# Cross attention: weights loaded a stage earlier, biases as one-row products, values placed by ScalarE

## The chip, the cores and the metric

The kernel runs on one core of a Trainium2 chip, in one launch. The metric is the device time of one execution in microseconds (us), lower is better. TensorE (PE) multiplies, VectorE (DVE), ScalarE (ACT) and GpSimd (POOL) work on vectors, SyncE (SP) issues most of the transfers. Each engine runs its own instruction list in order, and semaphores order the engines among each other.

## The reference, cut to what matters

Four gated layers run one after the other on x of 4x256x256, each one an attention-like part and a feed-forward part. The third attention-like part is the cross attention that the change touches; ahead of it stands a mixture of 16 experts with top-2 routing.

```python
x = x + jnp.tanh(g_ffn[1]) * _L1_ffn_ref(_layernorm(x, axis=-1), ...)            # 16 experts: stage 3
x = x + jnp.tanh(g_xattn[2]) * _L2_xattn_ref(_layernorm(x, axis=-1), ctx_1024, ...)  # stage 4
...
y_dca = y[:, -DCA:, :]                       # the last 16 of 256 context rows
y_main = y[:, :-DCA, :]
kv_dca = (y_dca @ Wkv_dca + bkv_dca).reshape(b, DCA, 2, H, HD)
k_dca = _ln(kv_dca[:, :, 0], kn_dca_w, kn_dca_b)
v_dca = kv_dca[:, :, 1]
q = _ln((x @ Wq + bq).reshape(b, s1, H, HD), qn_w, qn_b)
kv = jnp.concatenate([y_main @ Wk + bk, y_main @ Wv + bv], axis=-1)
kv = kv.reshape(b, s2, H, 2 * HD)
k = _ln(kv[..., :HD], kn_w, kn_b)
v = kv[..., HD:]
ctx = _attn(qT, k..., v...)                  # softmax over the 240 main rows
ctx_dca = _attn(qT, k_dca..., v_dca...)      # softmax over the 16 others
return (ctx + DCA_WEIGHT * ctx_dca) @ Wo + bo
```

There are 16 heads of 16 columns; `_ln` normalises each head's 16 numbers. All of it is float32.

## The kernel before, in words

The program is a chain of stages, each a block in which every engine has its own list, with all engines meeting between the blocks. Stage 3 is the mixture of 16 experts (`sparse_moe`), stage 4 the cross attention (`stage4`). The 1024 tokens are 8 tiles of 128 rows; a tile is called t, a batch of 256 rows b is two tiles. SBUF is split into large regions (regA, regC, regD), from which an `Arena` hands out pieces in order.

Stage 3 begins with a layer norm, the routing, a store of the normalised rows to DRAM (`h_rows`, issued by SP) and their gather by expert (POOL, L1373). It ends with the gathers of the results (L1379), the last additions to x on DVE (L1638, L1640) and ScalarE's two copies of weights for stage 5 (L1064, L1066). SP's list at its start is two weight loads for stage 5 (`load_w5`, L1032 and L1033) and then the two `h_rows` stores (L1354).

Stage 4 starts with a preparation and goes over into a loop over 64 heads. The preparation is what the change touches:

- SP issues fifteen loads, the weights wkv, wdca, wq and wo and the biases and norm weights spread over 128 partitions (L1710 to L1724).
- POOL copies the context's odd tiles into `ctxm` (main rows, zeros elsewhere) and `ctxd` (the 16 other rows, zeros elsewhere; L1738 to L1741), clears the padding of `qpad` and `kpad` (L1743), and sets the columns of ones (L1749, L1755).
- DVE and ScalarE do the layer norm of x (`norm_on_vector`, L145 to L158), PE turns it (`turn_on_tensor`, L175) and ScalarE copies it to `hT` (L1817).
- PE projects keys and values for two tiles per batch (`project_kv`: one 128x512 product for an even tile, L1888; two for an odd one, L1890 and L1891) and queries (`project_q`: four 128x256 products per batch, L1898). ScalarE copies each result from PSUM (`keep_kv` L1797, `keep_q` L1801). PE's order is kv(0), kv(1), the transposes of h, q(0), then kv, kv, q of batches 1, 2 and 3.
- POOL adds the biases in SBUF (`add_biases`, L1760 and L1762) and places the values with their row mask into `vaug` (`place_values`, L1772), the right-hand factor of the last product of the attention, together with the columns of ones.
- DVE normalises the heads: `center_heads` (L2030 to L2034), then ScalarE's squares (L1806), `variances` (L2038, L2042), ScalarE's root (L1811), `scale_heads` (L2048, L2050), `affine_heads` (L2058, L2060) and `pads` (L2071, L2073), which write `kpad` and `qpad` as float32r parts. ScalarE's list has the squares of batch 0 behind `keep_q(1)`.
- Once all four batches are projected and kept (`s_kve` 8, `s_qe` 4), PE turns the keys of batch 0 (`turn_heads`, L1919), ScalarE copies them (L1834) and then does the squares of batch 1; DVE normalises batch 1 and takes the maxima of the scores of batch 0 (L2082). From there on the order is a slot list written out by hand, 16 slots per batch.

Inside the head loop 13 scan steps of another layer ("late" steps) are woven in; their buffers lie over pieces that only the preparation uses (`early`), so SP, POOL and ScalarE wait for the preparation before the first of them.

## Time and profile before

| | us |
|---|---|
| median of 3 runs | 985.37 |
| lowest and highest of them | 981.57, 985.49 |
| the profiled execution | 986.16 |
| its span | 984.4 |
| mean granted TensorE clock | 0.821 |
| busy: PE, DVE, ACT, POOL | 679.4, 724.4, 333.7, 194.9 |

Times in the profile count from the span's start. Stage 3 lies at about 351 to 481, stage 4 begins at 483.0, its head loop at about 566. A line of a timeline is: start, duration, engine, line of the kernel, operation, out<-in, number of instructions, and in brackets how long the engine had been idle before and what released it. In the profile an engine is busy while it executes; waits are inferred from semaphores. A matmul's recorded duration overlaps the next one's, so its price in a sequence is the distance between starts.

### The profile page before, as it was taken

How to read it: one execution, taken by the hardware profiler on the slowest of the kernel's cores; microseconds unless marked ns; L12 is line 12 of the kernel's file. 1: busy time of each engine (PE TensorE's matmuls, PEld its weight loads, DVE VectorE, ACT ScalarE, POOL GpSimd, SP SyncE). 2: the span in 40 equal slices, each digit the busy share in tenths (PEclk: the TensorE clock that was granted, in tenths of full speed). 3: DMA queues.
4: the chain of work that ended last, by engine and by line, in shares of the span. 5: the costliest groups of instructions: out<-in, count | busy, mean ns of one | idle time of the engine just before them, and what ended most of it. 6: DMA issues, size and time to landing. Idle time of an engine off the chain costs nothing. (4 is left out here: it accounts for less than half of the span.)

```text
span 984.4 us, 9448 instructions
## 1 busy us (share of the span) xinstructions
PE 679.4 (69%) x3040; PEld 447.3 (45%) x3043; DVE 724.4 (74%) x1379; ACT 333.7 (34%) x534; POOL 194.9 (20%) x168
## 2 busy tenths in 40 slices
PE   4419989999945434898273388988861443489997
PEld 2304545555534333566142255555440222477775
DVE  5997798979866765966438769788849886945554
ACT  4004517455213311231232265555620322423221
POOL 0000001112200003343478000000104121204441
PEclk9758999999977665999586589789885675579999
DMA  9300003434574031453400033423625000000000
GB/s 238 90 12 0 6 0 65 85 65 85 88 198 138 0 129 43 112 126 93 108 16 0 0 86 78 91 58 75 139 45 202 0 1 0 10 0 1 22 1 22
DMA packets 39538, 62.22 MB, mean 63 GB/s; under 512 B 5010, under 2 KB 24090, under 8 KB 38210
## 3 DMA queue, kind: packets, MB, share of 16 engines
q1 hardware_dynamic: 28530, 38.68, 13.6%
q0 software_dynamic: 10960, 22.94, 12.7%
q8 instruction: 25, 0.41, 0.2%
q14 instruction: 23, 0.19, 0.1%
HBM read 38.54 MB, written 6.29 MB: 46 GB/s over the span
## 5 line engine op out<-in xcount | busy, mean ns | idle before, releaser
L519 PE MATMUL ps<-hT,regA 128*128 128x512 f32 x256 | 115.3, 593 | 1.0 <-ACT hT L435 1.0
L1975 PE MATMUL ps<-regD,regC 128*34 128x256 f32 x256 | 74.1, 416 | 23.2 <-ACT regD L1840 11.8
L519 PEld LDWEIGHTS ps<-hT,regA 128*128 128x128 f32 x256 | 48.4, 190 | 51.9 <-issue 46.8
L690 POOL DMA_DIRECT2D yssm<-regB x19 | 22.9, 1208 | 246.5 <-DVE regB L642 236.0
L530 PE MATMUL ps<-regA,regC 128*128 128x256 f32 x256 | 64.3, 396 | 6.9 <-DVE regC L649 5.4
L1149 POOL TENSOR_TENSOR w_lo<-regA,w_hi 128x768 fp32r<-128x768 f32 x22 | 42.6, 1940 | 100.1 <-ACT w_hi L1111 100.1
L530 PEld LDWEIGHTS ps<-regA,regC 128*128 128x128 f32 x256 | 47.9, 194 | 31.9 <-DVE regC L649 20.7
L1373 POOL DMA_INDIRECT regA<-h_rows,regA x31 | 30.1, 970 | 141.2 <-DVE regA L1593 110.9
L445 ACT ACTIVATE regC<-ps 128x512 f32<-128x512 f32 x32 | 19.1, 597 | 92.8 <-PE ps L519 88.1
L1840 ACT ACTIVATE regD<-ps 128x512 f32<-128x512 f32 x64 | 38.1, 596 | 32.9 <-PE ps L1961 32.1
L1287 DVE TENSOR_TENSOR regB<-regB,ps 128x512 f32<-128x512 f32 x22 | 15.1, 688 | 45.8 <-ACT regB L1129 45.8
L1975 PEld LDWEIGHTS ps<-regD,regC 128*34 128x34 f32 x256 | 24.8, 117 | 48.2 <-issue 18.9
L634 DVE TENSOR_TENSOR_SCAN regB<-regB 128x512 f32<-128x512 f32 x38 | 44.5, 1213 | 2.8
L1788 POOL DMA_DIRECT2D yssm<-regC x13 | 15.7, 1211 | 136.1 <-DVE regC L2123 114.4
L2082 DVE TENSOR_REDUCE regC<-ps 128x4 f32<-128x960 f32 x64 | 39.8, 685 | 3.9 <-PE ps L1930 3.9
L1919 PE MATMUL ps<-ident,regA 128*128 128x128 f32 x192 | 32.3, 339 | 14.9 <-DVE regA L2073 10.6
L175 PE MATMUL ps<-ident,h 128*128 128x128 f32 x112 | 20.5, 360 | 26.0 <-DVE h L158 25.1
L1919 PEld LDWEIGHTS ps<-ident,regA 128*128 128x128 f32 x192 | 29.2, 179 | 18.4 <-issue 11.7
L1174 PE MATMUL ps<-h_hi,w_hi 128*128 128x512 f32 x88 | 36.1, 410 | 0.0
L1174 PE MATMUL ps<-h_lo,w_hi 128*128 128x512 f32 x88 | 35.7, 405 | 0.0
L1174 PE MATMUL ps<-h_hi,w_lo 128*128 128x512 f32 x88 | 35.4, 403 | 0.0
L1467 PE MATMUL ps<-regB,regA 128*128 x124 | 35.1, 408 | 0.0
(375 smaller groups left out, 1720.5 us busy)
## 6 DMA issues: line engine op xcount, KB each, us to landing
yssm<-regB POOLq DMA_DIRECT2D x19, 512.0 KB, 5.0
regC<-bc_rows SPq DMA_DIRECT2D x26, 256.0 KB, 3.8
yssm<-regC POOLq DMA_DIRECT2D x13, 512.0 KB, 6.9
regB<-in_L_w SPq DMA_DIRECT2D x4, 1088.0 KB, 11.5
regA<-in_L_w SPq DMA_DIRECT2D x1, 4224.0 KB, 15.0
y_rows<-regA SPq DMA_DIRECT2D x31, 128.0 KB
regB<-in_L_w SPq DMA_DIRECT2D x1, 2176.0 KB, 13.0
regC<-in_L_W SPq DMA_DIRECT2D x2, 1024.0 KB, 5.9
```

The source lines that it names most:

```text
L519: m = nc.tensor.matmul(ps[:, 2 + 2 * (u % 2) + j, :], w[:, k * 2048 + c * P:k * 2048 + (c + 1) * P], hT[:, k, hf * HALF:(hf + 1) * HALF], ...
L530: m = nc.tensor.matmul(ps[:, t // 2, (t % 2) * D:(t % 2 + 1) * D], itm[:, u % 2, t * P:(t + 1) * P], WDv[:, c // 2, c % 2, :], start=(c == ...
L634: v.mark(nc.vector.tensor_tensor_scan(hs[:, k, :], dA[:, g % RD, k].rearrange("p b l -> p (b l)"), dBu[:, k, :], 0.0, ALU.mult, ALU.add))
L690: nc.gpsimd.dma_start(y, hc[:, g % 2], accum_op=ALU.add).then_inc(s_y, 16)
L1149: nc.gpsimd.tensor_tensor(wP[LO][:, u % RING, :], W[:, u % NC, :], wP[HI][:, u % RING, :].bitcast(F32), ALU.subtract).then_inc(s_wL, 1)
L1174: m = nc.tensor.matmul(ps[:, 2 + 2 * (u % 2) + j, :], wP[pw][:, u % RING, c0:c0 + P], hP[ph][:, k, hf * HALF:(hf + 1) * HALF], start=k == ...
L1373: nc.gpsimd.indirect_dma_start(xg[:, b % NG, :], None, h_rows, bass.IndirectOffsetOnAxis(rowid[:, b:b + 1], 0)).then_inc(s_got[b % NG], 16)
L1467: m = nc.tensor.matmul(ps[:, block_banks(u)[1], 0:GU], lhs, W[:, bass.ds(at + k * GU, GU)], start=k == 0, stop=k == KD - 1)
L1840: nc.scalar.activation(prob[:, n % 4, :], ps[:, 4 + n % 2, :], ACT.Exp, scale=SCALE4).then_inc(s_p, 1)
L1919: m = nc.tensor.transpose(ps[:, blk // 2, c0:c0 + P], flat(src[:, b % 2, t])[:, blk * P:(blk + 1) * P], ident[:, :])
L1975: m = nc.tensor.matmul(ps[0:VW, 6 + j % 2, (n % 2) * S:(n % 2 + 1) * S], vaug[:, 2 * b + kt, hd, :], prob[:, n % 4, kt * S:(kt + 1) * S], ...
L2082: nc.vector.tensor_reduce(dst[:, :, :, j], sc[:, :, :, lo:hi], AX.X, ALU.max, negate=True).then_inc(s_mx, 1)
```

## The change

- `load_w4` is new: eleven loads of stage 4 (wkv, wdca, the rows bkv, bdca and bq on one partition each, wq, mask, and the norm weights qn and kn) are issued by SP in stage 3, right behind `load_w5` and ahead of the `h_rows` stores, into the last 2816 words of regC, which stage 3 gives up. Stage 4 issues only bo and wo.
- The biases are no longer spread over the partitions and added by POOL. Each projection gets one more product that accumulates into the same PSUM bank: a left factor of one row (`ind`, ones and zeros that POOL writes) times the one-row bias. An even kv tile gets one product of 1 row x 512, an odd one two, each query tile one of 1 row x 256. That is 12 products of 512 columns and 8 of 256.
- `place_values` goes: ScalarE's `keep_kv` writes the values from PSUM straight into `vaug`, scaled by the mask column, once for an even tile and twice for an odd one, and then copies only the keys. `kv` is half as wide. POOL clears the second half of the even tiles' columns once.
- DVE's `center_heads` waits for ScalarE's copies, not for POOL. PE's first projection waits for the early loads, `ctxm`/`ctxd` and `ind`.

```diff
+        qn, kn, mask = sb("qn", [P, 2, 16]), sb("kn", [P, 2, 2, 16]), sb("mask4", [P, 2, 2])
...
+        s_w4 = ctx.enter_context(nc.semaphore("w4_loaded"))
+        NDCA = 16
+        NMAIN = S - NDCA
+        EARLY4 = 4 * D + 2 * D + 2 * 2 * D + D
+        REST_C = WORDS_C - EARLY4
+        early4 = Arena(regC[:, REST_C:])
+        wq4, wkv4, wdca4 = early4.take([KD, D]), early4.take([2 * D]), early4.take([2 * D])
+        brow4, bqrow4 = early4.take([2, 2 * D]), early4.take([D])
+
+        def load_w4(sp):
+
+            one = lambda nm, n: a[nm].partition_broadcast(n)
+            for dst, src in ((wkv4, a["q4_wkv"]), (wdca4, a["q4_wdca"]), (brow4[0:1, 0, :], one("q4_bkv", 1)),
+                             (brow4[0:1, 1, :], one("q4_bdca", 1)), (wq4, a["q4_wq"]), (bqrow4[0:1, :], one("q4_bq", 1)),
+                             (mask[:, :, :], a["q4_mask"]), (qn[:, :, :], one("q4_qn", P)), (kn[:, 0], one("q4_kn", P)),
+                             (kn[0:NMAIN - P, 1], one("q4_kn", NMAIN - P)), (kn[NMAIN - P:P, 1], one("q4_kd", NDCA))):
+                sp.dma_start(dst, src).then_inc(s_w4, 16)
+
+        LOADS4 = 11
...
+                        load_w4(sp)
...
-            sparse_moe("stage3", NE3, P, NB3, W3, UW3, rt3, 5, s_w3, 7, Arena(regA, regC), shared=True, bias=bias3,
+            sparse_moe("stage3", NE3, P, NB3, W3, UW3, rt3, 5, s_w3, 7, Arena(regA, regC[:, 0:REST_C]), shared=True, bias=bias3,
...
-            ar = Arena(regA, regD, regC)
+            ar = Arena(regA, regD, regC[:, 0:WORDS_C - 7 * T])
             qpad, kpad = ar.take([2, 2, NH, HC]), ar.take([2, 2, NH, HC])
-            kv = ar.take([NT, 2 * D])
+            kv = ar.take([NT, D])
             q = ar.take([NT, D])
             NG = 2 * NH
-            late = ar.take([7 * T])
+            late = regC[:, WORDS_C - 7 * T:]
             dAl = late[:, 0:2 * T].rearrange("p (r k b l) -> p r k b l", r=2, k=KD, b=2)
             rows_l = late[:, 2 * T:4 * T].rearrange("p (r j n) -> p r j n", r=2, j=2)
             dBl = late[:, 4 * T:5 * T].rearrange("p (k n) -> p k n", k=KD)
             hcl = late[:, 5 * T:7 * T].rearrange("p (r k n) -> p r k n", r=2, k=KD)
-            early = Arena(late)
+            early = Arena(late[:, 0:7 * T - EARLY4])
             sq = early.take([2, NG * HD])
             vaug = ar.take([NT, NH, VW])
             prob = ar.take([4, 2 * S])
-            wq, wkv, wdca, wo = early.take([KD, D]), early.take([2 * D]), early.take([2 * D]), ar.take([KD, D])
+            wo = ar.take([KD, D])
             ctxm, ctxd = early.take([B, P]), early.take([B, P])
-            bkv = early.take([2, 2 * D])
-            bq, bo = early.take([D]), ar.take([D])
-            qn, kn = ar.take([2, HD]), ar.take([2, 2, HD])
-            mask = ar.take([2, 2])
+            ind = early.take([3, P])
+            bo = ar.take([D])
...
-                    sp.dma_start(wkv, a["q4_wkv"]).then_inc(s_wk, 16)
-                    sp.dma_start(wdca, a["q4_wdca"]).then_inc(s_wk, 16)
-                    sp.dma_start(mask, a["q4_mask"]).then_inc(s_w, 16)
-                    sp.dma_start(wq, a["q4_wq"]).then_inc(s_w, 16)
-                    row = lambda nm: a[nm].partition_broadcast(P)
-                    sp.dma_start(bkv[:, 0, :], row("q4_bkv")).then_inc(s_w, 16)
-                    sp.dma_start(bkv[0:NMAIN - P, 1, :], a["q4_bkv"].partition_broadcast(NMAIN - P)).then_inc(s_w, 16)
-                    sp.dma_start(bkv[NMAIN - P:P, 1, :], a["q4_bdca"].partition_broadcast(NDCA)).then_inc(s_w, 16)
-                    sp.dma_start(bq, row("q4_bq")).then_inc(s_w, 16)
-                    sp.dma_start(bo, row("q4_bo")).then_inc(s_w, 16)
-                    sp.dma_start(qn, row("q4_qn")).then_inc(s_w, 16)
-                    sp.dma_start(kn[:, 0], row("q4_kn")).then_inc(s_w, 16)
-                    sp.dma_start(kn[0:NMAIN - P, 1], a["q4_kn"].partition_broadcast(NMAIN - P)).then_inc(s_w, 16)
-                    sp.dma_start(kn[NMAIN - P:P, 1], a["q4_kd"].partition_broadcast(NDCA)).then_inc(s_w, 16)
+                    sp.dma_start(bo, a["q4_bo"].partition_broadcast(P)).then_inc(s_w, 16)
                     sp.dma_start(wo, a["q4_wo"]).then_inc(s_w, 16)
                     sp.wait_ge(s_qs, B)
-                    sp.wait_ge(s_kb, 3 * B)
+                    sp.wait_ge(s_kve, NT)
+                    sp.wait_ge(s_qe, B)
...
+                    nc.gpsimd.memset(ind[0:1, 0, :], 1.0).then_inc(s_ind, 1)
+                    for r, (lo, hi) in ((1, (0, NMAIN - P)), (2, (NMAIN - P, P))):
+                        nc.gpsimd.memset(ind[0:1, r, lo:hi], 1.0).then_inc(s_ind, 1)
+                        rest = (hi, P) if lo == 0 else (0, lo)
+                        nc.gpsimd.memset(ind[0:1, r, rest[0]:rest[1]], 0.0).then_inc(s_ind, 1)
+                    nc.gpsimd.memset(vaug[:, 0::2, :, HD + 1:2 * HD + 1], 0.0).then_inc(s_va, 1)
                     for v_ in (qpad, kpad):
                         nc.gpsimd.memset(v_.rearrange("p a t g d -> p (a t g) d")[:, :, KS:HC], 0.0).then_inc(s_va, 1)
-                    pool.wait_ge(s_va, 2)
-                    pool.wait_ge(s_w, 16 * 12)
+                    pool.wait_ge(s_va, 3)
+                    pool.wait_ge(s_w4, 16 * LOADS4)
                     for t in range(2):
                         for j in range(4):
                             ones = kpad[:, :, t, :, KS + j]
                             nc.gpsimd.tensor_scalar(ones, ones, mask[:, t, j % 2:j % 2 + 1], None, ALU.add).then_inc(s_va, 1)
-                    pool.wait_ge(s_va, 10)
+                    pool.wait_ge(s_va, 11)
                     for par in range(2):
                         for j in range(2):
                             c0 = j * (HD + 1) + HD
                             ones = kpad[:, 0, par, :, KS + j].unsqueeze(1).broadcast_to([P, NT // 2, NH])
                             nc.gpsimd.tensor_copy(vaug[:, par::2, :, c0], ones).then_inc(s_va, 1)
 
-                    def add_biases(b):
-                        for t in (2 * b, 2 * b + 1):
-                            pool.wait_ge(s_kve, t + 1)
-                            nc.gpsimd.tensor_tensor(kv[:, t, :], kv[:, t, :], bkv[:, t % 2, :], ALU.add).then_inc(s_kb, 1)
-                        pool.wait_ge(s_qe, b + 1)
-                        nc.gpsimd.tensor_tensor(q[:, 2 * b:2 * b + 2, :], q[:, 2 * b:2 * b + 2, :],
-                                                bq.unsqueeze(1).broadcast_to([P, 2, D]), ALU.add).then_inc(s_kb, 1)
-
-                    def place_values(b):
-                        pool.wait_ge(s_kb, 3 * (b + 1))
-                        for t in (2 * b, 2 * b + 1):
-                            for j in range(2):
-                                mk = mask[:, t % 2, j:j + 1]
-                                src = kv[:, t, :].rearrange("p (g d) -> p g d", d=HPAD)[:, :, HD:HPAD]
-                                c0 = j * (HD + 1)
-                                nc.gpsimd.tensor_scalar(vaug[:, t, :, c0:c0 + HD], src, mk, None,
-                                                        ALU.mult).then_inc(s_va, 1)
-
-                    add_biases(0)
-                    add_biases(1)
-                    place_values(0)
-                    add_biases(2)
-                    add_biases(3)
-                    for b in range(1, B):
-                        place_values(b)
...
                     def keep_kv(t):
                         act.wait_ge(s_kv, t + 1)
-                        nc.scalar.copy(kv[:, t, :], ps[:, t % 4, :]).then_inc(s_kve, 1)
+                        both_ = ps[:, t % 4, :].rearrange("p (g d) -> p g d", d=HPAD)
+                        for j in range(1 + t % 2):
+                            if t == 0 and j == 0:
+                                act.wait_ge(s_w4, 16 * LOADS4)
+                            c0 = j * (HD + 1)
+                            nc.scalar.activation(vaug[:, t, :, c0:c0 + HD], both_[:, :, HD:HPAD], ACT.Copy,
+                                                 scale=mask[:, t % 2, j:j + 1]).then_inc(s_vp, 1)
+                        nc.scalar.copy(kv[:, t, :].rearrange("p (g d) -> p g d", d=HD), both_[:, :, 0:HD]).then_inc(s_kve, 1)
...
                         if t % 2 == 0:
-                            m = nc.tensor.matmul(ps[:, t % 4, :], ctxT[:, t * P:(t + 1) * P], wkv, start=True, stop=True)
+                            nc.tensor.matmul(ps[:, t % 4, :], ctxT[:, t * P:(t + 1) * P], wkv4, start=True, stop=False)
+                            m = nc.tensor.matmul(ps[:, t % 4, :], ind[0:1, 0, :], brow4[0:1, 0, :], start=False, stop=True)
                         else:
-                            nc.tensor.matmul(ps[:, t % 4, :], ctxm[:, t // 2, :], wkv, start=True, stop=False)
-                            m = nc.tensor.matmul(ps[:, t % 4, :], ctxd[:, t // 2, :], wdca, start=False, stop=True)
+                            nc.tensor.matmul(ps[:, t % 4, :], ctxm[:, t // 2, :], wkv4, start=True, stop=False)
+                            nc.tensor.matmul(ps[:, t % 4, :], ctxd[:, t // 2, :], wdca4, start=False, stop=False)
+                            for r in range(2):
+                                m = nc.tensor.matmul(ps[:, t % 4, :], ind[0:1, 1 + r, :], brow4[0:1, r, :], start=False,
+                                                     stop=r == 1)
                         m.then_inc(s_kv, 1)
 
                     def project_q(b):
                         pe.wait_ge(s_hT, b + 1)
                         for t in (2 * b, 2 * b + 1):
+                            o_ = ps[:, 4 + b, (t % 2) * D:(t % 2 + 1) * D]
                             for k in range(KD):
-                                m = nc.tensor.matmul(ps[:, 4 + b, (t % 2) * D:(t % 2 + 1) * D],
-                                                     hT[:, k, t * P:(t + 1) * P], wq[:, k, :], start=k == 0, stop=k == KD - 1)
+                                nc.tensor.matmul(o_, hT[:, k, t * P:(t + 1) * P], wq4[:, k, :], start=k == 0, stop=False)
+                            m = nc.tensor.matmul(o_, ind[0:1, 0, :], bqrow4[0:1, :], start=False, stop=True)
                         m.then_inc(s_q, 1)
 
-                    pe.wait_ge(s_wk, 32)
+                    pe.wait_ge(s_w4, 16 * LOADS4)
+                    pe.wait_ge(s_ctx, 4)
+                    pe.wait_ge(s_ind, 5)
                     project_kv(0)
-                    pe.wait_ge(s_ctx, 4)
                     project_kv(1)
                     turn_on_tensor(pe, h, 4, s_h, lambda t: t + 1, s_hTp)
-                    pe.wait_ge(s_w, 16 * 12)
...
-                            pe.wait_ge(s_va, NSET + NVB * (b + 1))
+                            pe.wait_ge(s_va, NSET)
+                            pe.wait_ge(s_vp, NVB * (b + 1))
...
-                        dve.wait_ge(s_kb, 3 * (b + 1))
+                        dve.wait_ge(s_kve, 2 * (b + 1))
+                        dve.wait_ge(s_qe, b + 1)
...
+                        dve.wait_ge(s_w, 32)
```

## Rows read from the trace of the kernel before

**Rows 1.** Waits of 480 to 570 us: waiter, releaser, us in total, times, longest.

```profile
DVE regC L2030 <- POOL regD L1762: 15.5, 1, 15.5
```

**Rows 2.** Timeline of stage 4's start.

```profile
483.55 0.15 POOL L1739 MEMSET regC<- 128x64 f32 x1
...
484.05 0.23 POOL L1741 COPY regC<-ctxT 128x64 f32<-128x64 f32 x1
484.22 1.83 POOL L1743 MEMSET regA<- 128x1024 f32 x2
...
486.46 2.07 PE L1888 MATMUL ps<-regC,ctxT 128*128 128x512 f32 x2 [22.41 <-DMA regC<-in_q_wdca]
...
489.05 0.42 SPq L1724 DMA_DIRECT2D regD<-in_q_wo  x1
...
490.69 1.91 PE L175 MATMUL ps<-ident,h 128*128 128x128 f32 x16
...
497.04 3.78 PE L1898 MATMUL ps<-regC,hT 128*128 128x256 f32 x8 [4.44 <-DMA regD<-in_q_wo]
497.18 2.96 POOL L1749 TENSOR_SCALAR regA<-regA,regC 128x32 f32<-128x32 f32 x8 [11.13 <-DMA regD<-in_q_wo]
```

**Rows 3.** Timeline of batch 0's head normalisation and the keys' transposes.

```profile
505.36 0.69 DVE L2030 TENSOR_REDUCE regC<-regA 128x32 f32<-128x512 f32 x1 [15.53 <-POOL regD L1762]
...
525.55 3.65 PE L1919 MATMUL ps<-ident,regA 128*128 128x128 f32 x16 [10.55 <-DVE regA L2073]
```

**Rows 4.** Timeline of batch 1's head normalisation, up to the first maxima.

```profile
526.93 0.68 DVE L2030 TENSOR_REDUCE regC<-regA 128x32 f32<-128x512 f32 x1
...
531.05 0.65 ACT L1806 ACTIVATE regC<-regA 128x512 f32<-128x512 f32 x1
...
541.47 9.65 DVE L2082 TENSOR_REDUCE regC<-ps 128x4 f32<-128x960 f32 x16
```

**Rows 5.** Two lines of the source alone: ns min/median/max, first and last start.

```profile
L2058 DVE TENSOR_TENSOR regA<-regA,regC x8: 666/693/1636, 516.7 to 648.1; 128x512 f32<-128x512 f32 x8
...
L1801 ACT COPY regD<-ps x4: 586/586/599, 500.9 to 515.0; 128x512 f32<-128x512 f32 x4
```

**Rows 6.** PE's timeline: one batch of projections, start to start.

```profile
506.23 1.02 PE L1888 MATMUL ps<-regC,ctxT 128*128 128x512 f32 x2
...
510.53 1.02 PE L1888 MATMUL ps<-regC,ctxT 128*128 128x512 f32 x2
```

**Rows 7.** PE's timeline around products of 8 rows in an earlier stage.

```profile
103.29 0.59 PE L519 MATMUL ps<-hT,regA 128*128 128x512 f32 x1
...
103.81 1.98 PE L502 MATMUL ps<-regB 8*128 8x512 f32 x4
...
105.72 0.48 PE L530 MATMUL ps<-regA,regC 128*128 128x256 f32 x1
...
106.04 0.59 PE L530 MATMUL ps<-regA,regC 128*128 128x256 f32 x2
```

**Rows 8.** Chain that ended last, last stage: a 40-row product among 128-row ones.

```profile
885.54 2.75 PE ps L1174 x12
888.29 0.43 PE ps L1185
```

**Rows 9.** One-microsecond windows: busy of PE, PEld, DVE, ACT, POOL; PEclk; DMA.

```profile
489.00:490.00 1.00, 1.00 (x3) 0.51 (x2) 0.83 (x3) 0.16 (x1) 0.00 (x0) 0.70 0.57 157
...
503.00:504.00 1.00, 1.00 (x3) 0.43 (x2) 0.00 (x0) 0.40 (x1) 1.00 (x2) 0.87 0.00 0
...
520.00:521.00 1.00, 0.00 (x0) 0.00 (x0) 0.97 (x2) 0.00 (x0) 1.00 (x1) 0.66 0.00 0
```

**Rows 10.** Stage 3's row store by line, its landing in the page, the first gather.

```profile
L1354 SPq DMA_DIRECT2D h_rows<-h x2: 365/371/377, 356.8 to 358.0; - x2
...
h_rows<-h SPq DMA_DIRECT2D x2, 512.0 KB, 4.3
...
380.81 1.09 POOL L1373 DMA_INDIRECT regA<-h_rows,regA  x1 [110.89 <-DVE regA L1593]
```

More of the change, by code:

```diff
@@ L1643, in stage3 @@
         def stage3():
[L1644 removed]
+            sparse_moe("stage3", NE3, P, NB3, W3, UW3, rt3, 5, s_w3, 7, Arena(regA, regC[:, 0:REST_C]), shared=True, bias=bias3,
                        with_w5=True)
[L1650 removed]
+        NH, HD = 16, 16
         HPAD = 2 * HD
         SCALE4, EPS4 = HD ** -0.5, 1e-6
[L1653 removed]
         VW = 2 * (HD + 1)
@@ L1688, in stage4 @@
             part = cnt1[:, :].rearrange("p (c d) -> p c d", d=HD)
-            (s_var, s_sd, s_h, s_hTp, s_hT, s_wk, s_w, s_v, s_q, s_qe, s_kv, s_kve, s_kb, s_qv, s_qs, s_sqi, s_sq, s_kp, s_qp, s_T, s_Te,
+            (s_var, s_sd, s_h, s_hTp, s_hT, s_ind, s_w, s_v, s_q, s_qe, s_kv, s_kve, s_vp, s_qv, s_qs, s_sqi, s_sq, s_kp, s_qp, s_T, s_Te,
              s_s1, s_mx, s_qm, s_s2, s_p, s_pv, s_pe, s_pt, s_o, s_oP, s_oT, s_fin, s_ctx, s_va) = (
-                sem("s4_" + n) for n in ("var sd h hTp hT wk w v q qe kv kve kb qv qs sqi sq kp qp T Te s1 mx qm s2 p pv pe pt o oP oT "
+                sem("s4_" + n) for n in ("var sd h hTp hT ind w v q qe kv kve vp qv qs sqi sq kp qp T Te s1 mx qm s2 p pv pe pt o oP oT "
                                          "fin ctx va").split())
@@ L1695, in stage4 @@
             groups = lambda w: w.rearrange("p t (g d) -> p (t g) d", d=HD)
-            kview = kv.rearrange("p t (g d) -> p (t g) d", d=HPAD)[:, :, 0:HD]
+            kview = groups(kv)
             wide = lambda c: c.unsqueeze(2).broadcast_to([P, NG, HD])
             NHB = B * NH
-            NSET, NVB = 2 + 8 + 4, 4
+            NSET, NVB = 2 + 8 + 4 + 1, 3
             TK, TQ, MAX0, TM = 0, 2, 4, 13
@@ L2005, in _ @@
                     pe.wait_ge(s_oT, 4)
+                    pe.wait_ge(s_w, 32)
                     for t in range(NT):
@@ L2016, in _ @@
                     norm_on_vector(dve, v, s_var, s_sd, s_h)
-                    dve.wait_ge(s_w, 16 * 12)
+                    dve.wait_ge(s_w4, 16 * LOADS4)
                     dve.wait_ge(s_va, NSET)
@@ L2053, in affine_heads @@
                     def affine_heads(b):
-                        keys = kv[:, 2 * b:2 * b + 2, :].rearrange("p t (g d) -> p t g d", d=HPAD)[:, :, :, 0:HD]
+                        keys = kv[:, 2 * b:2 * b + 2, :].rearrange("p t (g d) -> p t g d", d=HD)
                         queries = both(b)[1][1]
```

3 lines of the change are left out of this document (removed).

## The prediction, written before the changed kernel ran

> **What bounds the kernel now.** The chain of waits that ended last reaches back only into the last stage, so it says nothing of stage 4; I went by three other views. First the list of waits over stage 4's preparation. Its largest entries that hold up work are DVE waiting for POOL's bias addition [rows 1] and PE waiting for loads. Then the timeline, to see in which order these waits end. PE gets its first weights at 486.46 and projects and turns until 492.6, then stands 4.4 us for the last of the loads and resumes at 497.04 [rows 2]. DVE has finished the layer norm by 490 and starts normalising heads only at 505.36, behind POOL's addition; it ends with the key pads of batch 0 at 525.5, and PE's transposes of the keys start at 525.55, released by DVE [rows 3]. PE has no work for 10.55 us before that, since its last projection (515.0). So the preparation is bound by loads, then POOL, then DVE. After 525.55 the path goes through ScalarE's squares of batch 1 (531.05) and DVE's normalisation of batch 1 to the first maxima at 541.47, from where DVE runs without a gap [rows 4]. The number to forecast is therefore when the transposes of the keys start, and how long they take. The third view is PE's own: starts record by record, to price the added products.
>
> **What goes.** Two waits for loads (to 486.46 and to 497.04), POOL's 12 additions and 16 placements. While POOL adds two SBUF operands, DVE's operation on two SBUF operands takes up to 1.64 us instead of 0.69 [rows 5]; that stretch goes too. If nothing took their place DVE would get to the key pads far earlier, and that is what one would bank on. What takes their place is PE.
>
> **When PE starts.** It needs `ctxm`/`ctxd` and `ind`. POOL ends the first at 484.05 + 0.23 = 484.3. The five writes of `ind` are on one partition and short: at 0.15 each, like a 64-column clear, 0.75 [rows 2]. PE starts at 485.0, 1.5 us earlier than now.
>
> **PE's columns.** One batch now takes 510.53 - 506.23 = 4.30 us from start to start at the full clock [rows 6]: three products of 512 columns and four of 256, five units, 0.86 each. The change makes it 6 products of 512 and 6 of 256, nine units: 7.74. A product of one row costs as much as one of 128: the four records of 8x512 span 1.98 with 0.59 of it the last one's own, so three steps in 1.39, and all but the first of them 0.43 like those of 128 rows [rows 7]. Four batches are 4 x 7.74 = 31.0, the 16 transposes of h stay at 1.9 [rows 2]: 32.9 us.
>
> **The change of height.** This is the term that the edit hides. In the rows of the 8-row group the step from the last 128-row record (103.29) to the second record behind the group (106.04) is 2.75 us; five steps of 512 columns at 0.43 and one of 256 at 0.215 would be 2.365. So going to 8 rows and back costs 0.385, 0.19 a change: the first weight load behind a change isn't hidden under the product before it, while between products of one height it is [rows 7]. A second case agrees in direction: a single-pass 40-row product takes 0.43 to the next start, where its 128-row neighbours take 2.75/12 = 0.23 [rows 8]. The changed kernel goes to one row and back once per kv tile and once per query tile, 16 times, 32 changes: 16 x 0.385 = 6.2 us. Bounds: 0 (no row has a height of 1), and 6.4 from the 40-row case (0.43 - 0.23 = 0.2 a change, 32 x 0.2). I take 6.2; the 8-row products are float32 like these.
>
> The Trainium skill ("TensorE: Matmul & The Clock Gate", Part 3, The mechanism) says that a weight load overlaps running products only when its row group differs. The trace does not agree for products of equal height, whose loads are hidden [rows 6]; it does for a change of height. By the page's rule and its load time of 128 columns (columns/1.2, an estimate of 0.107 us), the 40 added loads would cost 4.3 us in place of 6.2.
>
> **The clock.** PE comes out of a long idle time at 1.2 GHz. At the first start (486.46) the granted clock rose at 489.6, 3.1 us later (a second at 0.70 is 0.6 us at half); at the second (497.04) it rose at 503.3, 6.2 us later [rows 2, 9]. Work done meanwhile loses half of that: 1.6 to 3.1 us, I take 2.3. Behind it PE has no idle stretch, so one such ramp remains where there are two now.
>
> **Sum.** 485.0 + 32.9 + 6.2 + 2.3 = 526.4 for the end of the last query product. ScalarE's copy is 0.59 [rows 5], with its two handovers 0.7: the transposes start at 527.1 (526.4 to 527.9), **1.5 us later than now**. Two checks that nothing else is later. ScalarE: behind kv(1) it has three half-size operations and the first copy of `hT`, at most 4 x 0.59 = 2.4 against the 1.9 of the transposes, so at most 0.5 on PE. DVE: the last query product of batch 0 ends at 485.0 + 5.2 + 1.9 + 2.6 + 4 x 0.385 + 2.3 = 498.5, so centering begins at 499.1 instead of 505.36 and takes 2.8 (526.93 to about 529.8). But the squares of batch 0 stand behind `keep_q(1)` in ScalarE's list: 498.5 + 7.7 + 1.5 + 0.6 = 508.4. From squares to pads takes at most 10.4 (531.05 to 541.47), so the pads are done by 518.8, and batch 1 is centred by 521.6 [rows 3, 4]. DVE is 5 us early: its relief is real and is not what ends last. POOL's columns of ones: 484.3 + 0.75 + three clears of 0.92 + 2.96 + four small copies, before 493, ahead of 499.1 [rows 2].
>
> The transposes of the keys take 3.65 us now because PE had idled and the clock had fallen (at 520.3, 5.3 us after its last projection); 16 transposes of the same shape at the full clock took 1.91 [rows 2, 3, 9]. In the changed kernel they come 0.7 us after a busy stretch: **1.7 us less**, straight on the path through ScalarE's copies to the squares of batch 1. Then all is as now: evacuation, squares, normalisation, maxima. Net: +1.5 - 1.7 = **-0.2 us** (-0.9 to +0.6, to +1.1 with ScalarE's half microsecond).
>
> **Stage 3.** SP issues eleven loads ahead of the `h_rows` stores. The stage begins at about 351 and its two loads come first, so they start at about 352; at 0.42 (the row of L1724) to 0.5 each [rows 2] the last is out at 357.5, so the first store moves from 356.8 by under a microsecond. It lands in 4.3, the second by 363, and the first gather is at 380.81, released by DVE's row numbers [rows 10]: 18 us to spare. Cost 0; without the cover, 5 to 10 us. Stage 3's other work doesn't touch the tail of regC. In the head loop nobody waited for POOL's placements in the list of waits; 0.
>
> The profiled execution took 986.16 (span 984.4); the median is 985.37, and I apply the difference to it: **985.2 us**. A measurement here can tell about 0.5%, 4.9 us, from no change.
>
> **Rivals.** *A change of height to one row is free.* Speaks for it: I have two cases of other heights and none of one row. Then the transposes start at 520.9 and the sum is -6.4: 979.0. Half of it hidden: -3.3, 982. *PE stays at 1.2 GHz through the one-row products* (the slower side). Place: the stretch from 485.0 to the last query product. Against it: the clock stood at full through the 8-row group at 104 us, as the 0.43 between its records shows. In full it would be 39.1 us of work taking almost twice as long, up to +32, near 1017. It decides for slower from about 7 us more at half clock on: 3.5 for the work and 1.7 if the transposes start slow. *The moved loads delay the experts' gather*: it needs the stores to land 18 us later, with eleven small and middle transfers in front of them; from there each microsecond counts, some 990 at worst. *The change does nothing since DVE is still the last*: it would need DVE's chain to be 5 us longer than worked out; the sum would be the same within 1 us, so it is counted with the forecast.
>
> **Chances.** Forecast, no change (983.5 to 987 on its own): 0.62. Free change of height: 0.17. Half hidden: 0.10. Clock: 0.05. Stage 3 or something that a longer list brings: 0.06. Faster by over 0.5%: 0.15 of the free case and 0.03 of the half: 0.18. Slower: 0.10. Same: 0.72. The range takes in the half-hidden case and the better part of the free one, and on the other side the early part of the clock case: 979.0 to 988.0.
>
> **What would show it.** Right: first projection at about 485.0; one batch of projections about 9.3 us from start to start, 7.7 of columns; gaps of 0.1 around each one-row product; PE busy without a pause to 526.4, the transposes released by ScalarE's last query copy and taking about 1.9; squares of batch 0 waiting for PE, not DVE; the maxima beginning within 1 us of 541.5. Wrong: 7.7 us a batch (the height costs nothing) or a PEclk of 0.5 in the middle of the projections; transposes released by DVE; a first gather later than 381.

## The result: 1.7% slower, because TensorE's clock falls

The changed kernel takes 1003.67 us in the median of 4 runs (996.14 to 1010.19), the kernel before beside it 985.43 (981.57 to 986.73): a ratio of 1.0171 (95% interval 1.0128 to 1.0214). The forecast was 985.2 in a range of 979.0 to 988.0. The outcome lies outside it, on the side of the rival that had been given 0.05. The profiled execution took 996.14 with a span of 994.4, so it shows the lower end of what the change costs: 10.0 us of the 18.2 between the medians. The longer runs come up again with the second profile of the change and with the products of 8 rows. Comparisons leave out runs more than 1.5% above a kernel's fastest, which takes one run of four from one experiment below and two of four from another.

The first view is the timeline of the changed kernel at the start of stage 4 and over its projections. It answers to [rows 2, 6].

```profile
480.57 2.71 DVE L146 BATCH_NORM_STATS2 lnst<-x 128x6 f32<-128x256 f32 x8 [2.76 <-PEq L66]
...
482.10 0.18 POOL L1753 MEMSET regC<- 1x112 f32 x1
...
482.43 2.04 PE L1882 MATMUL ps<-regC,ctxT 128*128 128x512 f32 x2 [18.86 <-POOL regC L1753]
...
491.61 1.97 PE L176 MATMUL ps<-ident,h 128*128 128x128 f32 x16
...
496.73 1.12 PE L1882 MATMUL ps<-regC,ctxT 128*128 128x512 f32 x2
497.79 1.12 PE L1883 MATMUL ps<-regC 1*128 1x512 f32 x2
...
506.03 1.12 PE L1882 MATMUL ps<-regC,ctxT 128*128 128x512 f32 x2
...
517.26 2.08 PE L1882 MATMUL ps<-regC,ctxT 128*128 128x512 f32 x2
519.26 2.07 PE L1883 MATMUL ps<-regC 1*128 1x512 f32 x2
...
533.84 1.22 PE L1898 MATMUL ps<-regC 1*128 1x256 f32 x2
535.78 3.64 PE L1918 MATMUL ps<-ident,regA 128*128 128x128 f32 x16 [0.72 <-issue]
```

Read the start times of L1882. From batch 1 to batch 2 they are 9.30 us apart, as forecast. From 506.03 to 517.26 it is 11.23, and the last batch takes 17.8. The same product of 512 columns (two records) has 1.12 at 496.73 and 2.08 at 517.26. Nothing is idle in between: from 482.43 to the transposes no record of PE has a wait. What differs between the two stretches is the clock. The windows of one microsecond show when, with the columns of [rows 9]:

```profile
489.00:490.00 1.00, 1.00 (x3) 0.29 (x2) 0.00 (x0) 0.00 (x0) 0.45 (x2) 0.89 0.00 0
...
513.00:514.00 1.00, 1.00 (x3) 0.43 (x2) 1.00 (x2) 0.17 (x1) 0.00 (x0) 0.56 0.00 0
514.00:515.00 1.00, 1.00 (x3) 0.81 (x3) 0.93 (x4) 0.00 (x0) 0.00 (x0) 0.50 0.00 0
...
530.00:531.00 1.00, 1.00 (x3) 0.35 (x3) 0.00 (x0) 0.00 (x0) 0.00 (x0) 0.50 0.00 0
```

The number behind POOL's share is the granted clock (0.89 in the first line). It rises at 489.2 and falls to 0.50 (1.2 GHz) at 513.1 while PE is busy for the whole of every microsecond. It stays there beyond the last projection. The first maxima and the normalisation of batch 1 follow from that; this is the timeline of DVE and ScalarE, which answers to [rows 3, 4]:

```profile
497.56 1.28 DVE L2032 TENSOR_REDUCE regC<-regA 128x32 f32<-128x512 f32 x2 [8.96 <-ACT regA L1796]
...
507.80 1.22 DVE L2040 TENSOR_REDUCE regC<-regC 128x64 f32<-128x1024 f32 x1 [7.40 <-ACT regC L1801]
...
535.10 0.58 ACT L1796 COPY regA<-ps 128x512 f32<-128x512 f32 x1 [5.21 <-PE ps L1898]
...
542.47 1.22 DVE L2040 TENSOR_REDUCE regC<-regC 128x64 f32<-128x1024 f32 x1 [22.68 <-ACT regC L1801]
...
551.62 9.65 DVE L2084 TENSOR_REDUCE regC<-ps 128x4 f32<-128x960 f32 x16
```

DVE is early, as forecast, and then stands 22.68 us for PE and ScalarE. Where DVE waited 15.5 us for POOL before [rows 1], it now waits for PE. From the stage's start the transposes of the keys begin at 535.78 - 480.57 = +55.2 us (before +42.5), the maxima at +71.05 (before 541.47 - 483.05 = +58.4): 12.6 us later. The stage began 2.5 us sooner than before, and the rest is equal (442.8 us from the maxima to the end, 442.9 before): 12.6 - 2.5 - 0.1 = 10.0, the difference of the two spans.

### The profile page after: what moved, and what is told of

Same layout as the page of the kernel before. It is cut to its first block and busy times, and to the rows that moved or that the text cites. A ratio compares the mean times of both kernels' runs of the same rounds, so it can differ in the third digit from the quotient of the medians.

```text
span 994.4 us, 9526 instructions
## 1 busy us (share of the span) xinstructions
PE 710.7 (71%) x3080; PEld 456.5 (46%) x3083; DVE 717.0 (72%) x1379; ACT 336.2 (34%) x546; POOL 161.4 (16%) x146
## 5 line engine op out<-in xcount | busy, mean ns | idle before, releaser
L1975 PE MATMUL ps<-regC,regD 128*34 128x256 f32 x256 | 74.1, 416 | 22.9 <-ACT regC L1835 12.9
L1150 POOL TENSOR_TENSOR w_lo<-regA,w_hi 128x768 fp32r<-128x768 f32 x22 | 42.5, 1936 | 99.9 <-ACT w_hi L1112 99.9
L446 ACT ACTIVATE regC<-ps 128x512 f32<-128x512 f32 x32 | 19.1, 597 | 92.8 <-PE ps L520 88.1
L1835 ACT ACTIVATE regC<-ps 128x512 f32<-128x512 f32 x64 | 38.0, 596 | 33.2 <-PE ps L1960 32.4
L1975 PEld LDWEIGHTS ps<-regC,regD 128*34 128x34 f32 x256 | 24.9, 117 | 48.0 <-issue 17.3
L1776 POOL DMA_DIRECT2D yssm<-regC x13 | 15.8, 1214 | 135.9 <-DVE regC L2125 120.3
```

Source lines behind the costliest of these rows:

```text
L1150: nc.gpsimd.tensor_tensor(wP[LO][:, u % RING, :], W[:, u % NC, :], wP[HI][:, u % RING, :].bitcast(F32), ALU.subtract).then_inc(s_wL, 1)
L1835: nc.scalar.activation(prob[:, n % 4, :], ps[:, 4 + n % 2, :], ACT.Exp, scale=SCALE4).then_inc(s_p, 1)
L1975: m = nc.tensor.matmul(ps[0:VW, 6 + j % 2, (n % 2) * S:(n % 2 + 1) * S], vaug[:, 2 * b + kt, hd, :], prob[:, n % 4, kt * S:(kt + 1) * S], ...
```

## The experiments

All comparisons below are with the kernel before, run beside them: 984.8 us for the first four labels (e1 to e4), 986.32 for the next four (e5 to e8), 985.32 for the last three. The first group ran on another chip than the two others, and the kernel before itself differs by up to 1.5 us between them.

### The changed kernel again

> The changed kernel a second time, for another execution of it: its runs so far fall into 996 to 998 us and 1009 to 1010 us. Theory (height): products of one row don't hold TensorE's clock up, and how long it stays at 2.4 GHz in the projections differs from one execution to the next; so an execution near 1009 has the clock low for most of the projections (transposes of the keys some 68 us behind the stage's start), one near 997 for their second half (55 us, as in the first trace). Rival (elsewhere): the slow executions lose their 12 us outside the projections, and these look the same in both.

1007.5 us (998.3 to 1011.78), ratio 1.0212 (1.0127 to 1.0297), so it is no accident of one run. The profiled execution took 1004.4 us, its span is 1002.6. The beginning of its stage 4 and its transposes:

```profile
487.69 2.71 DVE L146 BATCH_NORM_STATS2 lnst<-x 128x6 f32<-128x256 f32 x8 [2.73 <-PEq L66]
...
539.81 3.65 PE L1918 MATMUL ps<-ident,regA 128*128 128x128 f32 x16 [0.72 <-issue]
```

The clock is full from 497.6 to 521.5, is back from 531.7 to 535.1 and falls again. The transposes start at +52.1 and the maxima at +68.0, three microseconds earlier than in the profile of 996.14 us. So what the theory said of longer executions did not come in this one, and the rival did: of the 8.2 us by which its span is the longer one, 7.1 lie ahead of stage 4 and 4.2 behind the start of the maxima, and its preparation is 3.1 shorter. Common to both profiles are the fall in the middle of the projections and a preparation (stage start to maxima) that is longer than before, by 12.6 and 9.5 us. The fall comes in both; what the clock does behind it differs.

### Bias products of 128 rows

```diff
-(brow4[0:1, 0, :], one("q4_bkv", 1))
+(brow4[:, 0, :], one("q4_bkv", P))
...
-m = nc.tensor.matmul(ps[:, t % 4, :], ind[0:1, 0, :], brow4[0:1, 0, :], start=False, stop=True)
+m = nc.tensor.matmul(ps[:, t % 4, :], ind[0:128, 0, :], brow4[0:128, 0, :], start=False, stop=True)
```

and so for all twenty; `ind` keeps its ones in row 0 and has zeros in the 127 rows below. The columns that PE streams are the same.

> The same 20 bias products, but of 128 rows: the left factor has its ones in row 0 and zeros in the 127 others, and the biases are loaded onto all partitions. Same columns, no change of height. Theory (height): the clock rises 3 to 6 us behind the first product and stays at 2.4 GHz to the transposes; a batch of projections takes 7.7 us instead of 9.3; the transposes start 38 to 39 us behind the stage's start (55.3 in the changed kernel, 42.55 in the one before) and take 1.9; time about 979, 6 us under the kernel before. Rival (length): it is the longer list of products itself that lets the clock fall, then it falls here too and the time stays above 990.

981.35 us (10 runs, 974.43 to 984.43), ratio 0.994 (0.991 to 0.9969). PE's timeline, and then one window:

```profile
501.52 1.02 PE L1881 MATMUL ps<-regC,ctxT 128*128 128x512 f32 x2
502.38 1.02 PE L1882 MATMUL ps<-regC 128*128 128x512 f32 x2
...
509.26 1.02 PE L1881 MATMUL ps<-regC,ctxT 128*128 128x512 f32 x2
...
525.62 1.94 PE L1917 MATMUL ps<-ident,regA 128*128 128x128 f32 x16 [0.72 <-issue]
```

```profile
510.00:511.00 1.00, 1.00 (x4) 0.40 (x3) 0.00 (x0) 1.00 (x3) 0.00 (x0) 1.00 0.00 0
```

A batch takes 7.74 us, the nine units of the forecast without its 1.54 for the height. The stage began at 486.8 in this run, so the transposes start at +38.8, and they take 1.94 instead of 3.64. The clock is full from 494.6 to 535.5 without a fall. The added products have the same number and the same columns as in the change; only their height differs, and with it the time, by 26 us (1007.5 and 981.35, both beside 984.8).

### No biases

```diff
-nc.tensor.matmul(ps[:, t % 4, :], ctxT[:, t * P:(t + 1) * P], wkv4, start=True, stop=False)
-m = nc.tensor.matmul(ps[:, t % 4, :], ind[0:1, 0, :], brow4[0:1, 0, :], start=False, stop=True)
+m = nc.tensor.matmul(ps[:, t % 4, :], ctxT[:, t * P:(t + 1) * P], wkv4, start=True, stop=True)
```

> The changed kernel without its 20 bias products: the biases of queries, keys and values are left out of the result. It shows what the rest of the change is worth. Theory (height, and PE as the last): without them PE is done with the projections by about 504 and DVE is the last; the transposes of the keys start about 25 us behind the stage's start instead of 42.55, at the full clock, and the time is about 966. Rival (something else in the change costs, such as the earlier loads or ScalarE's placements): the time stays at 980 or above.

This kernel leaves the biases out of queries, keys and values. 965.99 us (962.08 to 966.96), ratio 0.9787 (0.9733 to 0.9841). The transposes start at +24.3, and DVE is what releases them:

```profile
505.26 1.94 PE L1913 MATMUL ps<-ident,regA 128*128 128x128 f32 x16 [1.08 <-DVE regA L2070]
```

So the rest of the change is worth about 19 us (984.8 - 966.0). The bias products take 15 of these when they have 128 rows (981.35 - 965.99), and more than all of them at one row.

### Few changes of height

In batches 1 to 3 the one-row products of a batch stand together at its front, ahead of the others that add to the same PSUM: two changes of height a batch in place of eight.

```diff
+nc.tensor.matmul(e_, ind[0:1, 0, :], brow4[0:1, 0, :], start=True, stop=False)
+for r in range(2):
+    nc.tensor.matmul(o_, ind[0:1, 1 + r, :], brow4[0:1, r, :], start=r == 0, stop=False)
+nc.tensor.matmul(ps[:, 4 + b, :], ind[0:1, 0, :], bq2[0:1, :], start=True, stop=False, skip_group_check=True)
+nc.tensor.matmul(e_, ctxT[:, 2 * b * P:(2 * b + 1) * P], wkv4, start=False, stop=True).then_inc(s_kv, 1)
...
```

> One-row products as in the change, but in batches 1 to 3 gathered into one run ahead of the 128-row products of the batch, the two query ones as one of 512 columns: the same columns of one-row products, 2 changes of height a batch instead of 8. Theory (height): the clock falls within the projections as before; the time is 3 to 5 us under the changed kernel's by the saved changes, still slower than the kernel before, 990 to 1005. Rival (gaps): what lets the clock fall are the short stops at each change of height; with a quarter of them it stays up and the time is near 982.

994.02 us (992.87 to 1002.26), ratio 1.0109 (1.0043 to 1.0176). PE's timeline of this kernel at its last batch, and then the windows there:

```profile
518.14 1.12 PE L1913 MATMUL ps<-regC 1*128 1x512 f32 x2
...
526.27 1.12 PE L1913 MATMUL ps<-regC 1*128 1x512 f32 x2
527.23 1.87 PE L1915 MATMUL ps<-regC 1*128 1x512 f32 x4
528.95 1.02 PE L1916 MATMUL ps<-regC 1*128 1x512 f32 x2
529.89 1.72 PE L1918 MATMUL ps<-regC,ctxT 128*128 128x512 f32 x2
```

```profile
529.00:530.00 1.00, 1.00 (x4) 0.24 (x2) 1.00 (x3) 0.00 (x0) 0.00 (x0) 1.00 0.00 0
530.00:531.00 1.00, 1.00 (x2) 0.53 (x3) 0.93 (x3) 0.00 (x0) 0.00 (x0) 0.64 0.00 0
```

The clock rises only at 499.6, 15.9 us after PE's first product. It falls at 503.0, 0.6 us into a pause of 1.25 us behind batch 0, is back at 516.6, falls again at 530.3, right behind a run of 3.6 us of one-row products, and is back at 533.7. At the second fall PE had been busy all the time, with two changes of height in the 8.13 us of the batch (518.14 to 526.27). So the small gaps at the changes are not what lowers it; the low products themselves are, which the next experiments check from the other side.

The transposes start at +55.1, as in the changed kernel's profile (+55.2): 33 us at half clock in place of 29, and the pause, cost about the 3.5 us that the fewer changes save in three batches. They take 1.94, with the clock up. The median is 13.5 us under that of the change beside it, against the 3 to 5 that the saved changes were to give; the preparation in the profile shows only 1.8 us of it (maxima at +69.2, +71.05 in the change), so most of that difference is not explained.

### Heights between: 32, 64, 2 and 8 rows

The edit is that of the 128 rows with another number. Rows below the first are zeros in each.

> The changed kernel with the twenty bias products and their ones 32 rows high instead of one (zeros below row 0), so that only the height differs from it and from the version with 128 rows. Theory (low products do not hold TensorE's clock, and the effect goes by the height): at 32 rows, a quarter of the height, the granted clock falls in the middle of the projections as with one row, the transposes of the keys start 50 to 55 us after the stage's start, and the time is 995 to 1010. Rival A (only a one-row product is special, as a degenerate case): the clock stays up, the changes of height still cost 0.19 each (6.2 us), the transposes start at about +45 and the time is 985 to 988. Rival B (the gaps at the changes of height make the clock fall): falls as with one row, and 64 rows fall too.

989.37 us (10 runs, 985.82 to 997.5), ratio 1.0037 (1.0005 to 1.0069). What the theory said of 32 rows did not come; rival A did. PE's timeline, and one window of the time in which the changed kernel has 0.50:

```profile
501.19 1.12 PE L1881 MATMUL ps<-regC,ctxT 128*128 128x512 f32 x2
502.24 1.12 PE L1882 MATMUL ps<-regC 32*128 32x512 f32 x2
...
510.49 1.12 PE L1881 MATMUL ps<-regC,ctxT 128*128 128x512 f32 x2
...
529.88 1.94 PE L1917 MATMUL ps<-ident,regA 128*128 128x128 f32 x16 [0.72 <-issue]
```

```profile
524.00:525.00 1.00, 1.00 (x3) 0.47 (x3) 0.24 (x1) 0.00 (x0) 0.00 (x0) 1.00 0.00 0
```

The batch is again 9.30 us, as with one row, and the clock is full from 494.0 to 534.9. The transposes start at 529.88 - 484.44 = +45.4. (The profiled run is the slowest of the ten; its extra time lies in the loop over heads, 202.1 us from the maxima to the next stage against 193.3 with 128 rows.) So the two costs come apart. The change of height costs its 6.2 us at 32 rows as at one: 4 x (9.30 - 7.74). The medians, each less that of the kernel before beside it, say +3.05 at 32 rows and -3.45 at 128, 6.5 apart. And only the low heights lose the clock.

> The same with 64 rows. Theory by height: half of the height may be enough or not; if the clock stays up, the 32 changes of height are all that is left against the version with 128 rows (981.35): +6.2 us, transposes of the keys at about +45, time 985 to 988. If it falls, 993 or more. Rival B (gaps at the changes of height make the clock fall, whatever the height): falls like one row, 995 to 1010, transposes at +50 to +55.

989.13 us (10 runs, 986.27 to 992.1), ratio 1.0035 (1.0008 to 1.0061): the same as 32 rows, and no fall once the clock is up. A batch takes 514.13 - 504.82 = 9.31. In the profiled run the clock rose only at 502.3, 16.3 us after PE's first product (7.4 with 32 rows), and the transposes start at +49.7, where +45 was expected. The 8.9 us more at half clock cost about 4.4 of that. Rival B, for which 64 rows had to lose the clock like one, falls.

> The changed kernel with bias products of 2 rows (ones in row 0, zeros in row 1). Theory by height (the lower the product, the less it does for the clock; 32 rows kept it, one row did not): 2 rows behave like one: the granted clock falls between 505 and 520, the transposes of the keys start at +50 to +55 from the stage's start, 995 to 1010. Rival (one row alone is a special case; two rows are like 32): the clock stays up, transposes at +45 to +47, 987 to 991.

1001.49 us (995.4 to 1010.84), ratio 1.0146 (1.0045 to 1.0248). The clock falls at 516.3, and the transposes start at +55.5:

```profile
538.94 3.65 PE L1917 MATMUL ps<-ident,regA 128*128 128x128 f32 x16 [0.72 <-issue]
```

> The same with 8 rows. Theory by height: between one row and 32; the clock falls in a part of the runs or later than with one row, 990 to 1005. Rival (one row alone is special): transposes at +45 to +47, 987 to 991.

1008.28 us in the median (994.98 to 1012.5), ratio 1.0158 (1.0043 to 1.0274), from the two lower runs of four. The profiled run is one of the others, 1010.04 us, and shows where their time goes. The windows, and then the transposes:

```profile
499.00:500.00 1.00, 1.00 (x4) 0.70 (x3) 0.00 (x0) 0.00 (x0) 0.00 (x0) 0.64 0.00 0
...
510.00:511.00 1.00, 1.00 (x3) 0.66 (x3) 0.00 (x0) 0.00 (x0) 0.00 (x0) 0.50 0.00 0
...
524.00:525.00 1.00, 1.00 (x3) 0.17 (x1) 1.00 (x3) 0.06 (x1) 0.00 (x0) 0.50 0.00 0
```

```profile
549.67 3.65 PE L1917 MATMUL ps<-ident,regA 128*128 128x128 f32 x16 [0.72 <-issue]
```

The clock is full for 10 us alone, from 499.7 to 510.0, in 65 us of unbroken work; the transposes start at +67.9, 12.7 later than in the changed kernel's profile. The expectation, a fall later than with one row or only in a part of the runs and 990 to 1005 us, was missed: in this profile the clock fell after 10 us at its full value, with one and two rows after 24. The rest of this run is that of the changed kernel's profile (stage 4 begins at 481.76, 442.8 us from the maxima to the end), so a later rise of the clock and an earlier fall are enough to bring 996 to 1010. Whether the runs of the change near 1010 come from this is open: none of them was profiled, and the one longer execution that was, 1004.4, had its extra time outside the preparation.

The rival that one row alone is a special case falls with these two. With zeros in all rows but one, 32 rows hold the clock and 8 don't, so it isn't the data either. Where between 8 and 32 it turns, or whether it turns gradually, was not tried.

### One-row products in one place of a batch

Only the two bias products of each odd tile have one row (8 of 20), the others 128. The edit is shown against the version with 128 rows:

```diff
-m = nc.tensor.matmul(ps[:, t % 4, :], ind[0:128, 1 + r, :], brow4[0:128, r, :], start=False,
+m = nc.tensor.matmul(ps[:, t % 4, :], ind[0:1, 1 + r, :], brow4[0:1, r, :], start=False,
```

> Bias products of the keys and values of the even tiles and of the queries 128 rows high, and only the two of each odd tile one row high: 8 of 20, 3.4 us of 38.8 us of columns, in four places. Theory (what counts is the share of low products in a stretch of PE's work): the clock stays up, and against the version with 128 rows only 8 changes of height are left: 8 x 0.19 = 1.5 us, transposes of the keys at +40 to +41, 982 to 985. Rival (any one-row product in the stretch makes the clock fall, however few): transposes at +45 to +52, 990 to 1000.

983.47 us (10 runs, 978.92 to 991.02), ratio 0.998 (0.9941 to 1.002). The clock rises at 487.2 and stays full to 524.8. Two starts of PE and the transposes:

```profile
502.44 1.02 PE L1881 MATMUL ps<-regC,ctxT 128*128 128x512 f32 x2
...
505.97 1.98 PE L1887 MATMUL ps<-regC 1*128 1x512 f32 x4
...
510.57 1.02 PE L1881 MATMUL ps<-regC,ctxT 128*128 128x512 f32 x2
...
519.59 1.94 PE L1917 MATMUL ps<-ident,regA 128*128 128x128 f32 x16 [0.72 <-issue]
```

8.13 us a batch is 7.74 and one pair of changes of height at 0.39; the transposes start at +40.2. So a one-row product as such does not lower the clock: this mixture of 8 among 20 holds it, where the change's own with all 20 does not.

### The kernel before with the loads moved and nothing else

`load_w4` is called in stage 3, as in the change, with 12 loads, the biases on all partitions.

```diff
+                        load_w4(sp)
...
-                    sp.dma_start(wkv, a["q4_wkv"]).then_inc(s_wk, 16)
...
-                    pool.wait_ge(s_w, 16 * 12)
+                    pool.wait_ge(s_w4, 16 * LOADS4)
```

> The kernel before with the loads of stage 4's weights, biases and mask moved to stage 3 (12 loads) and nothing else: POOL still adds the biases and places the values. Theory (the loads are worth what the waits for them cost, and the bias products gave it away): two waits of 4.4 us and 3.5 us for loads go, one rise of the clock is left instead of two, POOL starts its additions about 9 us sooner, the transposes of the keys start at +33 to +35 instead of +42.5, and the time is 975 to 979. Rival (POOL is what the preparation waits for, and its additions and DVE's shared operations stretch to fill the time): the transposes start at +38 to +42 and the time is 981 to 985.

976.55 us (974.68 to 983.18), ratio 0.9895 (0.985 to 0.994). PE starts its first product with the stage and the transposes come at +32.8:

```profile
481.81 2.05 PE L1894 MATMUL ps<-regC,ctxT 128*128 128x512 f32 x2 [17.29 <-PEq L66]
...
514.59 3.65 PE L1924 MATMUL ps<-ident,regA 128*128 128x128 f32 x16 [10.34 <-DVE regA L2079]
```

DVE releases them, as before, 10 us earlier. This part of the change alone gains 1.05%. In the forecast it doesn't show, because PE's added work takes its place.

### Biases in single-pass products of 128 rows

The bias rows are rounded to the single-pass float32 type by ScalarE, and the two bias products of the odd tile are one, with the ones of the tile's 112 main rows in row 0 of `ind` and those of the 16 others in row 32, against which the two biases lie: 16 products, no change of height.

```diff
+                    nc.scalar.copy(bh, brow4).then_inc(s_bh, 1)
+                    nc.scalar.copy(bhq[:, :], bqrow4).then_inc(s_bh, 1)
...
-                            for r in range(2):
-                                m = nc.tensor.matmul(ps[:, t % 4, :], ind[0:1, 1 + r, :], brow4[0:1, r, :], start=False,
-                                                     stop=r == 1)
+                            m = nc.tensor.matmul(ps[:, t % 4, :], ind[:, 1, :], bh, start=False, stop=True)
```

> The changed kernel with the bias products 128 rows high in single-pass float32 (the bias rows rounded to that type by a ScalarE copy), and the two bias products of the odd tile joined into one: 16 products instead of 20. Theory: no change of height, so the clock stays up as with 128 rows; a single-pass product of 512 columns takes 0.23 to the next start instead of 0.43 (and 0.86 for the pair of passes of a full float32 product), so the biases cost about 3 us instead of 13: the transposes of the keys start at +27 to +29 and the time is 968 to 972, within 3 to 5 us of the version without biases (965.99). Rival (a change of product type costs as a change of height does, or the clock falls at single-pass products): +34 or later, 975 or more.

967.65 us (965.97 to 973.49), ratio 0.9831 (0.9777 to 0.9884): the fastest of those that compute the whole of it, with rounded biases. PE's timeline:

```profile
499.29 1.02 PE L1887 MATMUL ps<-regC,ctxT 128*128 128x512 f32 x2
499.75 0.80 PE L1888 MATMUL ps<-bh,ind 128*128 128x512 f32 x1
500.38 1.02 PE L1890 MATMUL ps<-regC 128*128 128x512 f32 x2
...
504.29 1.02 PE L1887 MATMUL ps<-regC,ctxT 128*128 128x512 f32 x2
...
510.18 1.94 PE L1922 MATMUL ps<-ident,regA 128*128 128x128 f32 x16 [0.72 <-ACT regA L1801]
```

A batch takes 5.00 us where it took 4.30 without any bias product [rows 6]: the biases cost 0.7 a batch in place of 5.0, and the transposes start at +28.1.

## Why the prediction was wrong, by its own steps

**The step that failed** is in the part on the clock: "Behind it PE has no idle stretch, so one such ramp remains". It took for granted that PE's being busy keeps the clock up. The rows it had, of the clock falling after idle time [rows 9], and the 8-row group that ran at full clock [rows 7], are true; the inference was from four short products between 128-row ones to 20 products that make four of the nine units of a batch. The rival "PE stays at 1.2 GHz through the one-row products" named the place and the mechanism, and was set at 0.05 for that same group. It is what happened, in part of the stretch: from 513.1 to the last query product at 535.0, 22 us of work at half speed, so 11 us lost. With the first rise 6.8 us after the start, 3.4 us lost in place of 2.3, the sum is 1.9 + 32.9 + 6.2 + 3.4 + 11.0 + 0.7 = 56.1 from the stage's start; measured are 55.2. The transposes then took 3.64 instead of 1.9, so their gain of 1.7 us went as well: from their start to the maxima 15.8 us, before 15.9, and 14.1 with 128 rows. The rival's bound of some 7 us from which it decides for slower was passed.

The Trainium skill ("TensorE: Matmul & The Clock Gate", Part 1, What's actually happening) says that the clock is set by how busy PE has been lately, idle giving 1.2 GHz and busy 2.4. The trace does not agree for products of one row: PE is busy 1.00 in every window from 513 to 535, and the granted clock is 0.50 from 514 on. A reader who went by that sentence would have made the same error.

**What held.** *The start*: PE began 1.9 us after the stage's start, forecast 2.0. *The columns and the change of height*: 9.30 us a batch with one and with 32 rows, 7.74 with 128, 8.13 with one run of one-row products; so a pair of changes is 0.39, the 0.385 that was read from a single place [rows 7], and the 6.2 us hold, not the 4.3 of the prediction's other estimate. The rivals of a free or half hidden change fall. *DVE early*: centering began at 497.56 and waited for ScalarE's squares at both batches. *The transposes released by ScalarE's last query copy*, 0.7 us behind it. *Stage 3*: the eleven loads went out from 351.63 to 356.5; with the timeline of SP and POOL, which answers to [rows 10],

```profile
356.03 0.46 SPq L1317 DMA_DIRECT2D kn<-in_q_kd  x1
356.54 1.47 SPq L1376 DMA_DIRECT2D h_rows<-h  x2
```

```profile
380.37 1.08 POOL L1395 DMA_INDIRECT regA<-h_rows,regA  x1 [110.83 <-DVE regA L1615]
```

the stores went out when they had (356.54, before 356.8), landed in 6.9 us instead of 4.3, and the first gather started at 380.37, still for DVE's row numbers: cost 0, and the rival falls. With the clock held (128 rows) and the height unchanged, the forecast's sum without its 6.2 was 37.9 from the stage's start; measured are 38.8.

**What stays open.** Stage 4 began at 480.57 instead of 483.05. Over the eleven other profiles that start lies between 479.4 and 487.7, whatever the edit. Three of these microseconds are the first gather of stage 3, which comes 29.4 to 30.0 us after that stage's layer norm in seven profiles and 32.4 in six, but in the two compared here it is the early one both times. The difference is taken as scatter. The head loop scatters too, by 4 us in the second profile of the change and by 9 in that of 32 rows. So the profiles show 9.5 and 12.6 us of what the change costs in stage 4's preparation, and the rest of the 18.2 between the medians was not traced. Nothing was run between 8 and 32 rows, or between 8 and 20 one-row products. Each height has one profile, and for the heights that kept the clock ten run times beside it, none above 997.5. Why the clock's first rise came 16 us after PE's start in three profiles (8 rows, 64 rows, the grouped kernel) and 3 to 8 us after it in the others was not tested.

## What to carry to other kernels

A product of few rows costs its full columns and 0.19 us for each change to another height, and many of them in a stretch of work can cost half of PE's clock behind them as well: read the granted clock beside the busy time, since a busy PE is no evidence of a full clock. A constant that is to be added in PSUM is cheap as a product of all 128 rows, padded with zeros, in a single-pass type, if it may be rounded to that type. Before an engine is relieved of its work, do the other half alone (here the loads moved early, 1.05% by itself): the gain of the one part had been paid away by the other.

## What the runs showed of the hardware that was not expected

- TensorE at busy 1.00 drops from 2.4 to 1.2 GHz among products of 1, 2 or 8 rows (at 513.1, 516.3 and 510.0 us), and holds the full clock with 32, 64 and 128 rows of which all but one are zeros.
- The change of height costs the same 0.39 a pair at 1, 32 and 64 rows: it is no matter of how low the product is.
- At equal clock a product of 32 rows takes what one of 128 takes. The Trainium skill ("TensorE: Matmul & The Clock Gate", Why this matters for your kernels) says the same of a single product of 32 rows; the trace agrees, a batch at 32 rows being longer than one at 128 by the changes of height alone (9.30 and 7.74).
- The single-pass bias products cost 0.70 a batch (5.00 less 4.30) for two products of 512 and two of 256 columns: 0.23 per 512 columns, where the full float32 products have 0.86. With its other products at full float32 the kernel's clock did not fall before the transposes.
